# Mamba scan layer in fp32: the short convolution as narrow products on tap-stacked copies, projections in pieces, one place for two buffers, a deeper product ring

## The reference, cut to what matters

```
xz = x @ win.T;  u, z = jnp.split(xz, 2, axis=-1)          # 1024 channels each
uc = depthwise convolution of u, 4 taps, causal, + bconv
u = silu(uc)
dbc = u @ wx.T                                             # 32 step columns, 16 B, 16 C
delta = softplus(dt @ wdt.T + bdt);  A = -exp(Alog)
h = exp(delta*A) * h + (delta*u) * B                       # over the rows, 16 states a channel
y = (sum over states of h*C + u*Dp) * silu(z)
return y @ wout.T
```

## Time and profile before

| what | us |
|---|---|
| median of three runs | 8720.75 |
| the profiled execution: device time | 8726.59 |
| its span, first to last instruction | 8724.8 |
| setup, to the last copy of `comb` | about 89 |
| prologue, to the first scan of the loop | to 195.3 |
| loop over the chunks | 195.3 to about 7952 |
| final stage | to the end |

### The profile page before, as it was taken

How to read it: one execution, slowest core, us unless ns; L and a number is a source line. 1 busy time by engine, 2 the same in 40 slices (tenths; PEclk the granted TensorE clock), 3 DMA queues, 4 the chain that set the end, 5 groups by cost and what they waited for, 6 DMA issues and landing times. The chain is left out here.

```text
span 8724.8 us, 126052 instructions
## 1 busy us (share of the span) xinstructions
PE 7612.1 (87%) x29320; PEld 4286.0 (49%) x29320; DVE 8057.4 (92%) x11490; ACT 5108.1 (59%) x9098; POOL 7293.7 (84%) x4029
## 2 busy tenths in 40 slices
PE   7898988888898888888889888888888989887788
PEld 3555555554555555554555555455545555554333
DVE  1999999999999999999999999999999999997998
ACT  3666666666666666666666666666666666663111
POOL 1988988898998988898988988888989889884554
PEclk8998989899999999898989999898989999998888
DMA  5212222222212222222221222222222122222332
GB/s 179 71 63 89 91 90 88 86 81 86 88 64 68 90 93 90 86 87 76 90 90 51 81 91 91 90 87 85 78 88 77 60 88 90 91 88 96 105 106 82
DMA packets 348294, 757.22 MB, mean 87 GB/s; under 512 B 47776, under 2 KB 95776, under 8 KB 342752
## 3 DMA queue, kind: packets, MB, share of 16 engines
q1 hardware_dynamic: 337088, 743.08, 25.2%
q10 hardware_dynamic: 10400, 5.24, 0.2%
HBM read 684.89 MB, written 63.29 MB: 86 GB/s over the span
## 5 line engine op out<-in xcount | busy, mean ns | idle before, releaser
L480 POOL TENSOR_TENSOR dBu<-Bb,du 128x1024 f32<-128x1024 f32 x2048 | 4827.8, 2362 | 788.0 <-DVE hR L924 671.7
L924 DVE TENSOR_TENSOR_SCAN h<-dA,state,dBu 128x512 f32<-128x512 f32 x3328 | 4137.2, 1278 | 228.6 <-ACT dA L638 82.6
L638 ACT ACTIVATE dA<-delta,A 128x512 f32<-128x512 f32 x4096 | 2752.3, 689 | 1805.3 <-DVE h L924 1730.8
L771 PE MATMUL yT<-ident,hC 128*128 128x128 f32 x13312 | 2047.3, 298 | 650.0 <-DVE hC L936 648.8
L771 PEld LDWEIGHTS yT<-ident,hC 128*128 128x128 f32 x13312 | 1676.4, 152 | 1587.8 <-DVE hC L936 864.2
L936 DVE TENSOR_TENSOR hC<-h,Cb 128x512 f32<-128x512 f32 x3328 | 2223.4, 676 | 40.4 <-PE yT L771 40.4
L744 PE MATMUL bg<-hT,win_z 128*128 128x512 f32 x2048 | 1068.8, 671 | 0.0
L924 DVE TENSOR_TENSOR_SCAN hR<-dA,state,dBu 128x512 f32<-128x512 f32 x768 | 969.3, 1262 | 79.4 <-PE yT L771 79.4
L489 POOL TENSOR_TENSOR hR<-hR,Cb 128x512 f32<-128x512 f32 x768 | 978.5, 1274 | 0.0
L764 PE MATMUL bg<-comb,u 128*128 128x512 f32 x2112 | 952.2, 594 | 25.5 <-ACT sp_a L510 24.6
L728 PE MATMUL bg<-hT,win_u 128*128 128x512 f32 x2112 | 951.8, 593 | 0.9 <-ACT hT L522 0.9
(11 more groups left out here) (137 smaller groups left out, 7145.1 us busy)
## 6 DMA issues: line engine op xcount, KB each, us to landing
Bb<-bc_scratch SPq DMA_DIRECT2D x264, 512.0 KB, 7.3
Cb<-bc_scratch SPq DMA_DIRECT2D x264, 512.0 KB, 6.6
win_u<-in_win SPq DMA_DIRECT2D x264, 256.0 KB, 2.7
diag<-diag_scratch SPq DMA_DIRECT2D x264, 256.0 KB, 2.6
comb<-comb_scratch SPq DMA_DIRECT2D x33, 2048.0 KB, 9.9
win_z<-in_win SPq DMA_DIRECT2D x257, 256.0 KB, 2.7
part_scratch<-outev SPq DMA_DIRECT2D x132, 256.0 KB, 2.1
xin<-in_x SPq DMA_DIRECT2D x72, 256.0 KB, 6.1
```

The costliest lines, as they stand in the source:

```text
L480: pool.tensor_tensor(dBu[:, q % 2], Bb[:, 2 * q:2 * q + 2, :], du[:, j % 2, :].unsqueeze(1).broadcast_to([P, 2, T]), ALU.mult).then_inc(dB ...
L638: act.activation(dA[n % 3][:], delta[:, j % 2, :], ACT.Exp, scale=A[:, s, j * N + n:j * N + n + 1]).then_inc(dA_made, 1)
L771: ins = nc.tensor.matmul(yT[:, tt * P:(tt + 1) * P], product[:, tt * P:(tt + 1) * P], ident[:], start=first and tt == 0, stop=False, is_tr ...
L924: nc.vector.tensor_tensor_scan(to, dA[n % 3][:], dBu[:, q % 2, k, :], state[:, c:c + 1], ALU.mult, ALU.add).then_inc(h_made, 1)
```

## The change

1. **Convolution.** The u tile goes from PSUM to `pre` (two places) by ACT and from there to DRAM. Its last three columns go to `hist`, and from there to DRAM in front of the next chunk's tile. Four transfers bring it back as `tapped`: 32 channels x 4 taps on the partitions, 4 groups of 32 channels beside one another, 1 MB in all. PE then does four products of 128 x 32 weights (`wtap`), each to its own 32 partitions of one bank. The setup makes `wtap` on POOL instead of `diag` on ACT.
2. **One place.** `xin` and `tapped` lie in the two halves of `comb`. The halves of comb are loaded after the last use of each, one after C7 and one among the B and C loads. Output products take the second half first.
3. **Pieces.** U and Z are issued in two pieces, O and X in four, at new positions. D comes before Y at the start of a group, and D is taken one position after PE's instead of two.
4. **Ring.** `hC` has 8 places instead of 4.
5. **DVE.** In a pair with an aside state, the even state is saved before the product with C and the aside state after it, under a semaphore of its own. `row_shift` goes to POOL (with the sign handled by ACT).
6. **ACT.** The two `dA` of a pair no longer stand together: take_yT, the exponentials and z stand between them, and the other takes behind.
7. **POOL.** `steps` moves from pair 5 to pair 4, and `finish_u` by one position.

```diff
-HC, HR = 4, 2
+HC, HR = 8, 2
+GROUP = 32
+NG = P // GROUP
...
-    ("Y3", (32,)), ("D5", (32,)), ("U6", (33,)), ("Z4", (34,)), ("C5", (36,)), ("U7", (37,)), ("C6", (39,)),
+    ("D5", (32,)), ("Y3", (32,)), ("Z4", (33, 34)), ("C3", (34,)), ("U6", (35, 36)), ("C4", (37,)), ("U7", (37, 38)),
+    ("C5", (39,)),
...
-TAKE = {name: at[-1] + 2 for name, at in SCHEDULE}
+TAKE = {name: at[-1] + (1 if name[0] == "D" else 2) for name, at in SCHEDULE}
...
-        xin = sb("xin", [P, TT, D])
+        xin, tapped = comb[:, 0:TT, :], comb[:, TT:2 * TT, :]
+        pre, hist = sb("pre", [P, 2, T]), sb("hist", [P, MT, HALO])
...
+            def store_pre(par, m):
+                sp.dma_start(dram["pre"][par, m][:, HALO:], pre[:, m % 2, :]).then_inc(pre_stored[m % 2], 16)
+
+            def load_tapped(par, m):
+                rows = dram["pre"][par, m].rearrange("(j c) w -> c j w", c=GROUP)
+                for k in range(TAPS):
+                    sp.dma_start(tapped[k * GROUP:(k + 1) * GROUP, :, :], rows[:, :, k:k + T]).then_inc(tapped_loaded, 16)
...
+                        if p == AT[f"C{m}"][-1] + 1:
+                            sp.wait_ge(bg_ready, ready(i, f"C{m}"))
+                            if m + 1 < MT:
+                                load_wt(d1, m + 1)
+                                sp.wait_ge(pre_stored[(m + 1) % 2], i * 64 + ((m + 1) // 2) * 16 + 80)
+                                load_tapped(1 - s, m + 1)
...
-                            if q == 5:
+                            if q == 4:
                                 m, ms = (j + 1, s) if j + 1 < MT else (0, 1 - s)
                                 pool.wait_ge(dA_made, g * N + DU0)
                                 pool.wait_ge(dBu_made, g * NQ + 1)
                                 steps(g + 1, m, ms, i * MT + 2 * MT)
...
-                                if p == TAKE[f"C{m}"] + 4:
+                                if p == TAKE[f"C{m}"] + 3:
                                     finish_u(i + 1, 1 - s, m)
+                            if p == STATS_POS + 3:
+                                row_shift(i + 2)
...
+            def convolve(bank, c, m):
+                per = len(range(m % RING, MT, RING))
+                pe.wait_ge(wt_loaded[m % RING], (c * per + m // RING + 1) * 16)
+                pe.wait_ge(tapped_loaded, (c * MT + m + 1) * (16 * TAPS))
+                for j in range(NG):
+                    ins = nc.tensor.matmul(bank[j * GROUP:(j + 1) * GROUP, :], wtap[:, m % RING, j, :], tapped[:, j, :],
+                                           start=True, stop=True)
                 ins.then_inc(bg_ready, 1)
...
+                                if own == 1:
+                                    nc.vector.tensor_copy(state[:, j * N + n:j * N + n + 1],
+                                                          h[:, 0, T - 1:T]).then_inc(state_saved, 1)
+                                dve.wait_ge(hC_used, straight(g, n) - C0 + 1)
```

More of the change, by code:

```diff
@@ L67 @@
 AT = dict(SCHEDULE)
-TAKE = {name: at[-1] + 2 for name, at in SCHEDULE}
+TAKE = {name: at[-1] + (1 if name[0] == "D" else 2) for name, at in SCHEDULE}
+assert all(TAKE[name] <= POS - 1 for name in TAKE)
 BY_ACT = [name for name, at in SCHEDULE if name[0] != "Y"]
@@ L170, in _ @@
             act.wait_ge(skip_stored, 32)
-            for parity in range(2):
-                act.wait_ge(diag_stored[parity], 16 * TAPS)
         @block.tensor
@@ L424, in _ @@
             for k in range(RING):
-                for loaded in (wu_loaded, dg_loaded):
+                for loaded in (wu_loaded, wt_loaded):
                     sp.wait_ge(loaded[k], 16 * len(range(k, MT, RING)) * (CHUNKS + 1))
@@ L468, in _ @@
             steps(0, 0, 0, MT)
+            row_shift(1)
             with pool.Fori(0, CHUNKS // 2) as r:
@@ L634, in _ @@
                             p = j * NQ + q
-                            for n in (2 * q, 2 * q + 1):
-                                act.wait_ge(h_made, g * N + (n - 2 if n >= 3 else (0, -2, -1)[n]) + H0)
-                                act.activation(dA[n % 3][:], delta[:, j % 2, :], ACT.Exp,
-                                               scale=A[:, s, j * N + n:j * N + n + 1]).then_inc(dA_made, 1)
+                            step_dA(g, j, s, 2 * q)
                             if q == 1:
@@ L732, in convolve @@
-            def convolve(bank, c, m, s, taken):
-                per = len(range(m % RING, MT, RING))
-                pe.wait_ge(dg_loaded[m % RING], (c * per + m // RING + 1) * 16)
-                pe.wait_ge(bg_free, taken)
-                for k in range(TAPS):
-                    ins = nc.tensor.matmul(bank[:], diag[:, m % RING, k, :], u[:, s, m, k:k + T],
-                                           start=(k == 0), stop=(k == TAPS - 1))
-                ins.then_inc(bg_ready, 1)
-            def project_z(bank, j, slot, loads):
+                if ks[-1] == KD - 1:
+                    ins.then_inc(bg_ready, 1)
@@ L791, in background @@
                             continue
+                        part = lambda count: range(count // len(at) * piece, count // len(at) * (piece + 1))
                         if piece == 0:
@@ L948, in _ @@
+                                if own == 1:
+                                    last = hR[:, (j * NA + ASIDE.index(n + 1)) % HR, T - 1:T]
+                                    nc.vector.tensor_copy(state[:, j * N + n + 1:j * N + n + 2],
+                                                          last).then_inc(aside_saved, 1)
                             if p == STATS_POS:
                                 row_stats(i + 2)
-                            if p == STATS_POS + 4:
-                                row_shift(i + 2)
```

379 lines of the change are left out of this document (214 added, 165 removed), and 18 rows, old and new, of the table SCHEDULE.

## The result

The changed kernel took 8800.55 us (median of 4 runs, 8788.34 to 8804.63) beside 8721.67 us for the kernel before on the same chip: ratio 1.0088, 95% interval 1.0070 to 1.0105. It is slower by 0.9%, 79 us. The profiled execution has a span of 8802.8 us, against 8724.8 before.

What follows compares the result with a forecast made beforehand. The prediction took DVE to set the pace, with POOL nearly as full. Its terms, -33 us in the loop, +20 left over at the gate and +14 outside, gave +1 and a forecast of 8722 us, range 8670 to 8800.

Steps and rivals of the forecast that it cites:

- POOL's chain: POOL's delta and du before dBu of pair 5 make DVE wait 0.97 us a group, 2.02 in group 4: +251 us.
- before the first scan: Prologue +12 us and two more stores at the end of setup +2: +14 us.
- the state copies: On DVE, one copy instead of two before the next scan saves 0.06 us in aside pairs: -19 us, bounds 0 and -50.
- the waits for PE: DVE's waits for PE at hR, hC and the gate nearly all go as tiles are spread: -181 us.
- POOL at position 32: POOL's lateness of 1.12 us a chunk goes, since group 3 keeps one finish_u of three: -38 us.
- row_shift: Moved from DVE to POOL, 1.74 us each, 32 in the loop, less 0.3 each for a covered wait: -46 us.
- The rival that the chain costs nothing: POOL could overlap steps with something, so the 251 us would not come: about 8470 us, chance 0.10.
- the late round trip: Rival: tap load over about 9 us in the loop, C late on PE: +144 us, 8866 us, chance 0.10.
- The ring of 8 takes the 40.4 in any case: Deeper ring of products with C removes DVE's 40.4 us of waits for PE there.
- New order on ACT and PE, what is left: Gate waits left at group starts, 0.6 us a chunk: +20 us, bounds 0 and +64.
- The prologue: Each C waits for its 1 MB tap load, priced at 4.9 us, 6.3 to 8.8 a tile: +12 us with row_shift's +2.
- the case in which PE gains little or loses its clock: Rival: more PE backlog left, 2 us a chunk, prologue +30: 8784 us at most, 8750 in the middle, chance 0.22.

Runs made afterwards that it cites:

- the first experiment: Changed kernel with POOL's steps (delta, du) back behind dBu of pair 5 instead of pair 4: 8648.34 us, ratio 0.9914.
- Y first: Kernel with steps behind pair 5, plus Y ahead of D again on PE and D taken one position later: 8572.92 us, ratio 0.9827.
- a tile of 2.9 us: Changed kernel with every group of four narrow products issued three times over: 8890.68 us, ratio 1.0186.
- the take first: Kernel with steps behind pair 5, plus ACT's U, C, O or H take ahead of its second dA in pair 1: 8596.84 us, ratio 0.9851.
- The split alone: Kernel before, with only the state copies of aside pairs split, the straight one ahead of the product with C: 8670.22 us, ratio 0.9937.
- 64 columns: Changed kernel with the prologue's tap loads and narrow products cut from 512 to 64 columns, chunk 0 computed in part: 8765.36 us, ratio 1.0044.
- the fastest kernel: Changed kernel with steps behind pair 5, Y ahead of D, finish_u moved (third tile at 39), yT copied behind the second dA: 8449.02 us, ratio 0.9682.

## Why the prediction was right in its range and wrong in its sum

It forecast 8722 us, -13 in the loop and +14 outside, with a range of 8670 to 8800. Measured were 8800.55 us, +49 in the loop and +29 outside. That is at the very end of the range, and luck had a part in it: the end was set by a case of which only a part came true. The mechanism it named is right. Its sum is short by 108 us at the gate, by 15 in POOL's chain and by 15 before the first scan, and too high by 40 at the state copies and 13 at the waits for PE. In the table below each measured term is a difference of pair times, times 32; by rounding they add up to 2 more than the 79 of the medians.

| term | predicted | measured |
|---|---|---|
| POOL's chain, pairs 2 and 4 | +251 | +266 |
| waits for PE of before | -181 | -194 |
| POOL at position 32 | -38 | -38 |
| row_shift | -46 | -47 |
| state copies, pair 0 | -19 | -59 |
| left over at the gate, pair 1 | +20 | +128 |
| pair 7 of group 7 | 0 | -4 |
| before the first scan | +14 | +29 |
| sum | +1 | +81 |

*The mechanism was right and is shown.* The chain through POOL was forecast at 8.70 us and is 8.75. Taking it away took away its wait in all seven groups that had one. An undisturbed group gives 3.13 + 3.63 + 4.44 = 11.20 us for pairs 2 to 4 against 10.19 before, +1.01 where 0.97 was predicted; group 4 has 2.27 where 2.02 was predicted, with `finish_u` and du at 1.27 us instead of the 1.05 of the earlier trace rows. The rival that the chain costs nothing fell. So did the late round trip. The waits for PE at hR and hC went as said, and they stayed away in the first experiment, with a faster DVE. What took them away is by elimination the new schedule: neither the ring of 4 (in the kernel with steps behind pair 5 and Y first) nor a tile of 2.9 us brought them back. Each was tried alone and no run puts the tiles back to their old places, so the part of the schedule is argued and not shown. "The ring of 8 takes the 40.4 in any case" gave the ring what is gone without it too.

*The step that failed is "New order on ACT and PE, what is left".* It gave the gate 0.6 us a chunk, +20 us in all, with bounds of 0 and 2 a chunk. It is 4.0 a chunk: 0.95 in group 0, 0.95 in 3, 0.37 in 4, 1.31 in 5, 0.39 in 7, and nothing in group 1, where it was expected. The prediction had the facts for it. It said that Y "waits until the take two places before it, which stands behind that dA", but it priced this as a fixed path of 3.5 us behind PE's last product and then asked only for the backlog. The path doesn't start at PE's last product. Y's bank is freed by a take at a fixed place in ACT's order, behind the second dA of pair 1, and that dA waits for a scan. So Y is late without any backlog of PE, most where the tile two places ahead is C5, U3 or C2 (positions 41, 25, 33: 38.4, 20.5 and 11.1 us). The low clock adds to it: at 41 the gate waits 1.97 us in the mean with it and 0.90 without, and at 33 almost only with it. At position 1 (26.3 us) it was D in front of Y. The prediction had 0.6 a chunk for that, and D took 2.06 us there, at 1.2 GHz, where it takes 1.12 at full clock. Both experiments on this step, Y first and the take first, took the gate waits down, to none and to half.

*The state copies were mis-sized.* 0.06 an aside pair was predicted and 0.15 to 0.24 measured. From the start of the product with C to the next scan it was 0.91 us in pair 2 and 1.00 in pair 0. The prediction allowed 0.79 for it after the change and 0.06 for the copy ahead; the trace has 0.71 and 0.05. The split alone brings 55 us.

*The prologue was mis-sized*, +26 instead of +12. The load of a tile was priced at the x load's 4.9 us. The same bytes take 6.9 to 7.9 us when every row starts 4 bytes further on and a store and a weight load go with them, and a tile goes in 9.0 us, above the bound of 8.8. The last two tiles ran back to back before (the x16 in the earlier trace rows); now the last waits for its load like the others, which the prediction left out. With 64 columns the 29 us vanish. Which of the two makes the load slow was not tried.

Two statements of the Trainium skill were weighed in the prediction. By the Trainium skill's "TensorE: Matmul & The Clock Gate", Part 3, the estimate for a tile was 1.1 to 1.4 us, and it took 1.07 at full clock. By the Trainium skill's "TensorEngine Tiling (Array Packing)", Key Properties, a change of tiling mode should drain the engine. As idle time no such cost is seen: in the changed kernel's loop PE idled 9.2 us ahead of 2,048 narrow products, and 8.3 of these went to a load. It is seen in the starts. At full clock a U product starts 0.429 us after the one before it, but the first narrow product starts 0.523 us after the last U product (32 times), and behind the short products of yT 0.202 us instead of 0.109 (135 times). Behind a tile it is again 0.523. In the kernel before these steps were 0.429 and 0.109 at the convolution too. So a change costs about 0.09 us, two changes a tile, by estimate at most 48 us of PE in the loop (0.093 x 2 x 256). Whether this is a drain or a weight load that could not run ahead no run tells apart.

The range's upper end, 8800, came from the case in which PE gains little or loses its clock. The low clock had a part in what came, by the estimate above about half of the gate waits. But PE did gain, its mean clock in the loop stayed 0.92, the case's price for the rest was 2 us a chunk where the gate alone took 4.0, and its prologue was priced at +30. So the range held the time more by the width of this case than by its reasons. Open is what remains in the fastest kernel over the 28.1 us of an undisturbed group: 2.8 us a chunk in group 5 (row_stats), 2.6 in group 7 (turn of the loop), 1.6 in group 4 (POOL).

## What to carry to other kernels

Where two banks alternate, a product is released by the take of the tile two places ahead. Find where that take stands in the other engine's order and what that order waits for, before asking whether the producing engine has a backlog. An instruction moved one place earlier on a nearly full engine can be the costliest part of a change that is right in all else: here one line gave back 152 us, and with the order of Y and D, `finish_u` and yT mended as well the same change gains 3.2%. After each wait removed, look at the same places again, since the next one (here `finish_u`, then dA) stands a few rows further on.

## What the runs showed of the hardware

Products of 128x32 that write four different groups of 32 partitions run side by side. In the changed kernel's tile at 1845.67 the first four start within 0.02 us of each other and the other four 0.43 us later, and each is recorded with about 0.6 us. A tile's eight instructions take 1.07 us at full clock. The eight of a tile of full width held PE for 3.43 us in the earlier trace rows. A change between full-width and 32-column products put about 0.09 us between their starts.

How long PE had idled doesn't tell by itself which clock it then gets. At position 41 of the changed kernel PE idled 2.2 us ahead of Y in all 32 chunks. Y's two products then took 2.07 us in 6 of them, 1.3 to 1.8 in 4 and 1.12 to 1.17 in 22. At position 1 they took 2.07 in all 27 chunks in which they start there, whether PE had idled some 5 us just ahead of D or not at all.

Transfers of 256 KB with rows offset by 4 bytes had a median of 4.7 us from issue to landing, and the store of 256 KB before them 5.4. The store of the earlier trace rows had 2.1 in the kernel before and has 2.7 in this one, where the DMA engines are busy for 0.41 of the loop instead of 0.25, so a part of the longer times may be the traffic:

```profile
comb<-pre_scratch SPq DMA_DIRECT2D x1056, 256.0 KB, 4.7
...
pre_scratch<-pre SPq DMA_DIRECT2D x264, 256.0 KB, 5.4
```
